# Passage between two layers of a fused transformer program: TensorE flips the first tile of layer 2 right after the last weighted sums of layer 1, three projections move behind, and ScalarE and VectorE take their work of the passage in another order

## The reference, cut to what matters

```python
x = L0_attn_x                                   # (4, 1024, 128), float32
xn = _layernorm(x, axis=-1)
x = x + _L0_attn_ref(xn, ...) + _L0_ffn_ref(xn, ...)     # layer 1: 16 heads of causal attention, gated MLP
xn = _layernorm(x, axis=-1)
x = x + _L1_attn_ref(xn, ...) + _L1_ffn_ref(xn, ...)     # layer 2
...
# _L1_attn_ref: the 4 sequences are the 4 steps of a delta-rule scan, the 1024 rows its batch
h = (x - mu) * rsqrt(var + LN_EPS) * ln_w + ln_b
q, k, v, beta = split(h @ w_slow);  beta = sigmoid(beta)
q = sum_norm(elu(q) + 1);  k = sum_norm(elu(k) + 1)
step:  delta = b_t * (v_t - W @ k_t);  W = W + delta k_t^T;  out_t = W @ q_t
return x + out @ w_out
# _L1_ffn_ref: 8 experts, the best 2 of them for each row
probs = softmax(input @ Wg);  top 2, renormalised
out = sum over experts of score * (relu(input @ W1 + b1) @ W2 + b2)
```

## Time and profile before

| | |
|---|---|
| Median of 3 runs | 1457.05 us (1454.94 to 1458.81) |
| Time of the profiled execution | 1462.21 us |
| Its span, first to last instruction | 1460.4 us |
| Mean granted TensorE clock | 0.992 of full speed |
| Busy: TensorE, VectorE, GpSimd, ScalarE | 97%, 85%, 66%, 64% of the span |
| Layer 1 | from 0 to about 912 us |
| Passage | about 912 to 975 us |
| Layer 2 | the rest |

### The profile page before, as it was taken

One profiled execution on the slowest core, in us unless ns is written; L12 is line 12 of the kernel. 1 busy time (PEld: TensorE's weight loads), 2 busy tenths in 40 slices (PEclk: granted clock), 3 DMA queues, 4 the chain that ended last, 5 costly groups with the idle time before them and its releaser, 6 DMA issues.

```text
span 1460.4 us, 29494 instructions
## 1 busy us (share of the span) xinstructions
PE 1411.2 (97%) x10306; PEld 876.7 (60%) x10306; DVE 1244.5 (85%) x1966; ACT 929.8 (64%) x1862; POOL 968.8 (66%) x756
## 2 busy tenths in 40 slices
PE   8989999999999999999999998889999999999998
PEld 6745555555555555555555555456767676776777
DVE  7578888788887888878888787399999999999997
ACT  3357677676776767767667675447665675657552
POOL 5135555557555556555556555559999999999895
PEclk9999999999999999999999999999999999999999
DMA  8048877867878777787877868200000000000000
GB/s 192 1 102 206 192 180 171 197 164 188 193 170 193 168 188 188 179 192 165 199 184 184 191 172 195 70 1 1 1 8 8 1 8 1 8 9 1 8 1 15
DMA packets 77149, 164.13 MB, mean 112 GB/s; under 512 B 31410, under 2 KB 43724, under 8 KB 77004
## 3 DMA queue, kind: packets, MB, share of 16 engines
q1 hardware_dynamic: 77004, 162.24, 46.6%
HBM read 9.08 MB, written 2.10 MB: 8 GB/s over the span
## 4 chain that ended last, share of the span: by engine, by line
PE 83%; DVE 8%; issue 4%; POOL 3%; ACT 2%; DVEq 0%; POOLq 0%; ACTq 0%
PE accum L1111 17%; PE both L1045 13%; PE both L2805 8%; PE flips_all L1045 6%; PE flips_all L2828 5%; PE flips_all L1137 4%; PE misc L1009 4%; PE flips_all L1009 4%; PE flips_all L2817 3%; PE flips_all L2865 2%; PE flips_all L1022 2%; PE misc L1022 2%; PE accum L2817 2%; PE accum L2828 2%; PE flips_all L2851 1%
## 5 line engine op out<-in xcount | busy, mean ns | idle before, releaser
L462 POOL TENSOR_SCALAR big<-big,recip 128x384 f32<-128x384 f32 (+7 forms) x512 | 374.5, 746 | 405.7 <-DVE recip L714 405.4
L722 DVE STREAM_TRANSPOSE big<-big 128x896 f32<-128x896 f32 (+7 forms) x288 | 345.8, 1224 | 20.0 <-POOL big L462 19.3
L1111 PE MATMUL accum<-across,v_sb 128*64 128x256 f32 (+1 forms) x2560 | 282.1, 363 | 13.4 <-issue 13.3
L543 ACT ACTIVATE big<-both,neg_max 128x1024 f32<-128x1024 f32 (+3 forms) x256 | 242.2, 950 | 47.4 <-DVE neg_max L704 27.7
L704 DVE TENSOR_REDUCE neg_max<-both 128x1 f32<-128x1024 f32 (+3 forms) x256 | 248.6, 1012 | 25.1 <-PE both L1050 22.4
L1111 PEld LDWEIGHTS accum<-across,v_sb 128*64 128x64 f32 x2560 | 178.2, 137 | 140.6 <-issue 73.9
L1045 PE MATMUL both<-qk_sb 64*128 64x512 f32 (+3 forms) x1024 | 215.5, 539 | 9.9 <-ACT big L543 9.2
L543 ACT ACTIVATE big<-flips_all,neg_max 128x256 f32<-128x256 f32 (+3 forms) x256 | 132.0, 524 | 107.3 <-DVE neg_max L704 88.7
L2805 PE MATMUL both<-slow_sb,h_T 128*128 128x512 f32 x384 | 181.5, 600 | 7.5 <-DVE xnT L2318 4.4
L1613 POOL TENSOR_TENSOR prod<-xnT,qs 128x1024 f32<-128x1024 f32 (+3 forms) x32 | 180.1, 5635 | 11.1 <-DVE qs L2318 11.1
L704 DVE TENSOR_REDUCE neg_max<-flips_all 128x2 f32<-128x512 f32 (+3 forms) x128 | 102.2, 820 | 97.7 <-PE flips_all L1050 97.0
(11 more groups left out here) (230 smaller groups left out, 2419.7 us busy)
## 6 DMA issues: line engine op xcount, KB each, us to landing
across<-big SPq DMA_DIRECT2D x1024, 144.0 KB, 2.5
out<-x SPq DMA_DIRECT2D x8, 256.0 KB, 2.3
x<-in_L_attn_x SPq DMA_DIRECT2D x3, 512.0 KB, 5.6
slow_sb<-in_L_attn_w_slow SPq DMA_DIRECT2D x3, 512.0 KB, 7.8
w_qk<-in_L_attn_qkv_w SPq DMA_DIRECT2D x2, 512.0 KB, 6.2
xn<-in_L_ffn_W SPq DMA_DIRECT2D x1, 1024.0 KB
x<-in_L_attn_x SPq DMA_DIRECT2D x2, 256.0 KB, 3.1
qs<-in_L_attn_qkv_w SPq DMA_DIRECT2D x1, 512.0 KB, 6.5
```

Source lines behind the costliest of these rows:

```text
L462: pool.tensor_scalar(part, part, recip[:, u % 2, SLOTS.index(row), h:h + 1], 0.0, ALU.mult, ALU.add).then_inc(scaled, 1)
L543: last = act.activation(probs_of(row, h).rearrange("p b j k -> p j b k"), scores_of(row, h).rearrange("p (j b k) -> p j b k", b=MOVES, k=3 ...
L722: dve.transpose(part, part).then_inc(turned[group_of(row)], 1)
L1111: last = pe.matmul(dst, lhsT=values_of(u, j, h), rhs=keys_of(g, rows[n:n + 2], j, h), start=j == 0, stop=j == rows[n + 1])
```

## The change

Only orders change: every instruction of before is there once after, with the same operands.

On TensorE the second weighted sums of unit 31 come right after `project(0, 1, 0)`, with the flip of `nrm` behind them, then `project(0, 2, 1)`, the flip of `hat`, one `hidden` product and `make_small`; the join of these sums comes after that. `project(0, 0, 2)` goes behind the join and `project(0, 1, 2)` between the first two experts. ScalarE takes `exps(0, 1, 0)` ahead of the two norms, keeps the weighted sums and the flips before `exps(0, 2, 1)`, and copies the values later. VectorE takes `set_up` (a copy of 64 columns) and `sum_keys(0, 1)` earlier, and `keep(0, 2, 1)` behind the two sums.

```diff
@@ ScalarE
             exps(0, 1, 1)
+            exps(0, 1, 0)
             norm(0)
             second_norm(0)
-            exps(0, 1, 0)
-            keep_values(0, 0)
-            exps(0, 2, 1)
-            keep_values(0, 1)
             last_att(UNITS - 1, 1)
-            last_keep_join(UNITS - 1, 1)
             keep_nrm(0)
             keep_hat(0)
+            exps(0, 2, 1)
             act.wait_ge(*high_moved[1])
-            relu(0, 1, 1)
+            relu(0, 0, 0)
+            last_keep_join(UNITS - 1, 1)
             gates(0)
             betas(0)
-            relu(0, 0, 0)
+            relu(0, 1, 1)
+            keep_values(0, 0)
             relu(0, 0, 1)
+            relu(0, 2, 0)
             relu(0, 1, 0)
-            relu(0, 2, 0)
             exps(0, 2, 0)
+            keep_values(0, 1)
             relu(0, 2, 1)
@@ VectorE
             keep(0, 0, 0)
+            set_up()
             last_sums(UNITS - 1, GROUPS[0])
             last_variance(UNITS - 1, GROUPS[0])
             keep(0, 1, 1)
             keep(0, 1, 0)
+            sum_queries(0, 0)
+            sum_keys(0, 1)
             keep(0, 2, 1)
-            set_up()
-            sum_queries(0, 0)
             keep_small(0)
...
             mixing(0, 0)
-            sum_keys(0, 1)
             gather(0, 1)
@@ TensorE
             project(0, 1, 1)
             project(0, 1, 0)
+            last_weigh(UNITS - 1, 1, (0, 0, 4), (2, 0, 6))
+            flip_nrm(0)
+            project(0, 2, 1)
+            flip_hat(0)
+            hidden(0, 0, 0)
+            make_small(0)
+            last_join(UNITS - 1, 1)
             project(0, 0, 2)
-            project(0, 2, 1)
-            project(0, 1, 2)
-            last_weigh(UNITS - 1, 1, (0, 0, 4), (2, 0, 6))
-            last_join(UNITS - 1, 1)
-            flip_nrm(0)
-            flip_hat(0)
             hidden(0, 1, 1)
-            make_small(0)
             hidden(0, 0, 1)
-            hidden(0, 0, 0)
             hidden(0, 2, 0)
             hidden(0, 1, 0)
             expert(0, 0)
+            project(0, 1, 2)
             expert(0, 1)
             project(0, 2, 0)
```

## The result

The changed kernel took 1449.64 us in the median of six runs (1446.01 to 1454.73), the kernel before 1458.86 us beside it (six runs, 1454.94 to 1462.12). The ratio is 0.994 with a 95% interval of 0.9923 to 0.9957: 9.2 us by the medians, 8.8 by the ratio, where 9.0 had been forecast.

What follows compares the result with a forecast made beforehand. The passage was taken as bound by the order in which TensorE reaches the flips. A lead of 8.1 us plus 0.9 us of clock gave 9.0 us off the 1457.05 us median: 1448.0 us, range 1445 to 1452.5.

Steps and rivals of the forecast that it cites:

- The weighted sums: TensorE, unit 31: second sums start right behind project(0, 1, 0), 11.7 us earlier, good to -0.2 and +1.5 us.
- Flips, small logits, VectorE's start: Behind the sums: small logits there at 934.8; VectorE's block starts at 935.9, 11.2 us earlier.
- The waits that come next: VectorE waits 1.3 us at gather(0, 1) and 2.9 us at keep(0, 2, 0), leaving a lead of 8.1 us.
- Moving the key sums: VectorE: sum_keys(0, 1) moved into idle time takes 1.1 us out of the block.
- TensorE's wait at `project(0, 3, 2)`: TensorE's 2.67 us wait for VectorE shrinks to 1.1 us as TensorE makes up 1.6 us.
- The clock: Behind TensorE's shorter wait, projection and expert product run at full speed: 0 to 1.7 us more, 0.9 taken.
- The sum: Whole kernel: 8.1 us of lead plus 0.9 us of clock make 9.0 us off.
- The lead is kept: Layer 2, from 975 on: all three engines run 8.1 us ahead with unchanged lists and their old waits.
- the lead was not spent: Rival: new waits in layer 2 lose half the lead, 1453 us, or all, 1457; chance 0.08.
- nothing ran at half clock over a stretch: Rival: flips to project(0, 2, 0) all at half clock, 16 us of matmuls take 32, 1465 us; chance 0.02.
- the first rival: Clock falls where TensorE alternates with ScalarE, 935 to 949, 1.9 us each: 1449.9 to 1452.7 us; chance 0.14.

Runs made afterwards that it cites:

- experiment 8: Changed kernel plus 24 identity flips on TensorE ahead of expert 3, tile 2, layer 2; 531.8 us from the start of project(0, 1, 1) to the end, changed kernel 529.7.
- experiment 9: Changed kernel with a feature sum done twice more on VectorE, tile 2, layer 2; 531.4 us from project(0, 1, 1) to the end, changed kernel 529.7.
- experiment 10: Changed kernel with GpSimd's key product of unit 1 repeated, tile 2, layer 2; 531.2 us from project(0, 1, 1) to the end, changed kernel 529.7.
- Experiment 2: Changed kernel with exps(0, 1, 0) back behind the two norms on ScalarE; 1456.61 us, 0.9967 of the kernel before.
- Experiment 1: Changed kernel with sum_keys(0, 1) back ahead of gather(0, 1) on VectorE; 528.9 us from project(0, 1, 1) to the end, changed kernel 529.7.
- experiment 4: Changed kernel with project(0, 2, 0) earlier on TensorE and its exponentials earlier on ScalarE; 1448.62 us, 0.9918 of the kernel before.
- experiment 5: Changed kernel with the second join and its copy back right behind the weighted sums; 530.3 us from project(0, 1, 1) to the end, changed kernel 529.7.
- Experiment 3: Kernel before the change plus 24 identity flips filling TensorE's wait ahead of project(0, 3, 2); 1459.26 us, ratio 1.0001.
- experiment 7: Experiment 4's kernel with feature sums of the first two inverses and keep(0, 2, 0) earlier, gather(0, 2) later on VectorE; 1447.43 us, 0.9909 of the kernel before.
- experiment 6: Changed kernel with project(0, 0, 2) back ahead of the second weighted sums on TensorE; 532.0 us from project(0, 1, 1) to the end, changed kernel 529.7.

## Why the prediction was right, step by step

- **The weighted sums.** Forecast at T0 + 3.9, measured T0 + 4.3 in the profiled execution, where they wait 0.58 us, and 3.6 to 3.9 in eight others, whose transfers were there sooner. The lower bound of 3.7 was a tenth too high: the first matmul starts at T0 + 3.63 while the projection, busy for 3.70, drains.
- **Flips, small logits, VectorE's start.** T0 + 14.2 forecast and measured, by two errors that cancel: the sums were 0.4 us late, and behind them TensorE started each product 0.1 to 0.2 us before the last had drained, which the sum took off mostly further on. Experiments 8 to 10, the same up to tile 2 with the sums at T0 + 3.6 to 3.8, start the block at T0 + 13.5 to 13.6. Experiment 2 shows that this step rests on the exponentials ahead of the norms.
- **The waits that come next.** 1.3 and 2.9 us were forecast, 1.74 and 2.75 measured, at the two places named. The lead is 7.8 and not 8.1 us in this execution. With the sums earlier, experiments 8 to 10 have the mark at T0 + 44.6 to 44.7, a lead of 8.4 to 8.5: how soon unit 31's transfers land is worth some 0.6 us here. That the alternation and not VectorE's block is the chain is shown by experiments 1, 4 and 5.
- **Moving the key sums** was counted as 1.1 us out of the block, and VectorE was then made to wait for TensorE. Experiment 1 shows that the second half of this sentence eats the first: worth 0.
- **TensorE's wait at `project(0, 3, 2)`.** 1.1 us forecast, 1.32 measured in this execution; GpSimd's product at T0 + 44.8 forecast, 45.2 measured.
- **The clock.** This term was mis-sized: 0.9 us was half of the bounds 0 to 1.7, and the whole came. Behind the shorter wait both products ran at full speed; the second of the gathers 4 and 5 starts about 9.4 us earlier from T0 (983.89 - 921.68 = 62.2 against about 967.27 + 1.19 - 915.66 = 52.8), 1.6 more than the lead before it. Experiment 3 gets the same 1.6 us out of the kernel before by filling the wait.
- **The sum.** 7.8 + 1.6 = 9.4, of which 9.0 arrive. The other 0.4 us go at one place of layer 2, 367 us behind the mark, where VectorE starts a `keep` late (rows below). GpSimd's wait near 1364 is longer behind it, 4.55 us where it was 4.13. The kernel before and experiments 1, 3, 7 and 9 lack the pause, the changed kernel and experiments 2, 4, 5, 6, 8 and 10 have it; what makes it stays open. So the 9.0 is errors that cancel: a lead smaller by 0.3 and a loss of 0.4 against a clock term larger by 0.7.
- **"The lead is kept."** Right, for a reason that I had only half. I argued from VectorE's unbroken list. Experiments 8 to 10 show that none of the three engines has slack where it was loaded, in tile 2, and experiment 7 that a lead of VectorE and GpSimd counts only as far as TensorE has it. That the same holds at every place of layer 2 is not shown.

The `keep` of "The sum" in the changed kernel, and the same one in experiment 1:

```profile
1328.57 1.22 DVE L2318 SCALAR_TENSOR_TENSOR qs<-both,e_buf 128x1024 f32<-128x1024 f32 x1 [0.26 <-issue]
```

```profile
1338.91 1.22 DVE L2318 SCALAR_TENSOR_TENSOR qs<-both,e_buf 128x1024 f32<-128x1024 f32 x1
```

The pause is short and waits for nothing that the profile shows ("issue").

The rivals: in the profiled execution no fall of the clock came in the alternation, where the granted clock reads 1.00 throughout; the lead was not spent; nothing ran at half clock over a stretch. That the first rival stayed away is partly luck of this execution. In five others the product behind the one long pause, ahead of `expert(0, 2)`, ran at half clock (last section). But at that place the rival's price was wrong too: none of these falls moved the mark. The Trainium skill, TensorE: Matmul & The Clock Gate, in its part on the HAM clock gate, says that the throttled state is the default and activity releases it. The trace of experiment 2 agrees with 0.50 behind a wait of 2.61 us; behind the pauses of up to 0.78 us in the alternation the clock stayed at 1.00.

## What to carry to other kernels

- Where several engines are 97% full together behind a passage, the passage itself is a place to gain, and a lead is worth what the last of these engines has of it: work out the new start of each, not only of the one that waited before.
- Look first for work that stands ahead of the critical product in an in-order queue though nobody needs its result yet. Then price the moved product at its new place by what it covered there, not by its length alone: `project(0, 0, 2)` also hid a copy of 0.6 us.
- Count from an event just ahead of the change when single profiled executions are compared; the runs of this kernel differ by more in their first 920 us than most edits are worth.

## What the runs showed of the hardware that was not expected

**The same 920 us vary by 11 us.** T0 lies between 915.66 and 926.84 over the twelve profiled executions, although nothing ahead of it differs but `set_up` and, in the seventh, two sums more on VectorE, all in its idle time. Part of it goes with the granted clock in the set-up. A window early in the changed kernel, and the same of the kernel before:

```profile
18.00:30.00 12.00, 10.04 (x61) 7.57 (x61) 11.79 (x36) 5.04 (x7) 8.15 (x6) 1.00 1.10 217
```

```profile
18.00:30.00 12.00, 10.07 (x50) 6.81 (x49) 11.71 (x35) 4.81 (x7) 8.06 (x6) 0.86 1.20 217
```

There and in 60 to 80 and 90 to 110 the changed kernel's run had 1.00 and the run of before 0.86, 0.91 and 0.91. The three executions with 1.00 in all three windows, the changed kernel's and those of experiments 6 and 10, have the three earliest T0 (915.66, 918.75, 918.00). But the runs of experiments 1 and 4 had the same three falls as before and T0 of 926.84 and 920.71, so the falls don't explain all of it, and the rest stays open.

**The same wait, at either clock.** Ahead of `expert(0, 2)` TensorE waits 2.06 or 2.07 us in the changed kernel and in seven experiments. The product took 2.02 us in the changed kernel and in the second and fifth experiment, but 3.39 in the sixth, whose timeline row is, with a window of TensorE in it (granted clock 0.50):

```profile
952.42 3.39 PE L2828 MATMUL flips_all<-w_qk,hid 128*128 128x128 f32 x16 [2.07 <-ACT hid L1812]
```

```profile
953.00:954.00 1.00, 1.00 (x7) 1.00 (x6) 1.00 (x2) 0.00 (x0) 1.00 (x1) 0.50 0.00 0
```

In the first, eighth, ninth and tenth it took 3.03, 3.19, 3.42 and 2.86. The work of the passage ahead of it is the same in the last three of these and in the changed kernel, so which clock it gets can't be read from the length of the wait alone. It cost nothing at the mark: from `keep(0, 2, 0)`, which starts just ahead of that product, to the mark all five take 15.3 us, as the changed kernel does (945.61 to 960.88).

**From a landed transfer to TensorE.** The last traffic that the windows show in the changed kernel lies between 919.4 and 919.5, and the sums start at 919.95: about 0.5 us. The profile names no releaser for their wait of 0.58 us; that it is these transfers is read from the semaphore for which the sums wait.
